# Windowed attention on one core: the row maxima transposed ahead of the values, and their rows sent by ScalarE alone

## The reference

```python
qkv = x @ w_qkv
q, k, v = jnp.split(qkv, 3, axis=-1)
# to_win: [B, H=16, nw=16 windows, W=128, E=32]; k_ctx, v_ctx: the window before, itself, the one behind
scores = jnp.einsum('bhnqe,bhnke->bhnqk', q * scale, k_ctx)
scores = jnp.where(valid[None, None, :, None, :], scores, NEG)
attn = jax.nn.softmax(scores, axis=-1)
out = jnp.einsum('bhnqk,bhnke->bhnqe', attn, v_ctx)
...
x = x + _layernorm(_L0_attn_ref(_layernorm(x, axis=-1), L0_attn_w_qkv), axis=-1)
x = x + _layernorm(_L0_ffn_ref(_layernorm(x, axis=-1), L0_ffn_gate_w1, ...), axis=-1)
```

## Time and profile before

| what | value |
|---|---|
| runs | 2930.49, 2940.21, 2943.89 us (median 2940.21) |
| profiled execution | 2937.19 us, of it the span 2935.3 |
| granted clock of TensorE, mean | 0.993 of full speed |
| attention stage | about 560 to 1290 us |
| one step of it, burst to burst | 5.43 us (1060.94 to 1066.37) |

### The profile page before, as it was taken

How to read it: one execution, slowest core, us unless ns; L and a number is a source line. 1 busy time by engine, 2 the same in 40 slices (tenths; PEclk the granted TensorE clock), 3 DMA queues, 4 the chain that set the end, 5 groups by cost and what they waited for, 6 DMA issues and landing times.

```text
span 2935.3 us, 55438 instructions
## 1 busy us (share of the span) xinstructions
PE 2867.0 (98%) x20252; PEld 2378.8 (81%) x20252; DVE 1994.9 (68%) x3769; ACT 1727.5 (59%) x3385; POOL 853.4 (29%) x713
## 2 busy tenths in 40 slices
PE   8999999999999999989989999999999999999998
PEld 6888888788888887778767888788888888888886
DVE  5333333488888887888868766886768766796664
ACT  3222222377767776665636666866667666676666
POOL 1000000188888887974400000500005000040003
PEclk9999999999999999999989999999999999999999
DMA  6555555678788889959999866985769765895642
GB/s 215 184 174 171 183 186 194 221 191 199 196 198 199 198 201 216 227 180 399 389 394 333 286 208 207 354 319 200 254 212 404 265 205 199 289 399 196 232 137 86
DMA packets 361429, 697.10 MB, mean 237 GB/s; under 512 B 26576, under 2 KB 127056, under 8 KB 361184
## 3 DMA queue, kind: packets, MB, share of 16 engines
q1 hardware_dynamic: 335456, 629.63, 67.0%
q10 hardware_dynamic: 17424, 32.24, 3.1%
q0 software_dynamic: 8304, 31.98, 2.7%
HBM read 525.45 MB, written 167.78 MB: 236 GB/s over the span
## 4 chain that ended last, share of the span: by engine, by line
PE 83%; DMA 6%; DVE 4%; issue 3%; ACT 2%; POOL 2%; ACTq 0%; DVEq 0%; SPq 0%; POOLq 0%
PE a_acc L571 18%; PE e_acc L1407 7%; PE e_hid L1390 7%; PE e_hid L1391 7%; PE e_hid L1392 7%; PE e_acc L1409 7%; PE e_acc L1408 7%; PE a_ps_score L622 5%; PE a_ps_keys L641 5%; PE a_ps_out L670 5%; DMA a_q_st<-a_max_rows 3%; DMA a_gate_att<-o_scratch 3%; PE a_ps_out L678 2%; PE a_ps_turn L688 1%; POOL a_gate_x L1231 1%
## 5 line engine op out<-in xcount | busy, mean ns | idle before, releaser
L1780 DVE SCALAR_TENSOR_TENSOR e_part<-e_ring,e_g_cols,e_part 128x512 f32<-128x512 f32 x896 | 647.5, 778 | 5.7 <-DMA e_ring<-mix_rows 3.2
L487 DVE TENSOR_REDUCE a_neg_max<-a_ps_score 128x1 f32<-128x384 f32 (+1 forms) x1024 | 490.1, 526 | 48.8 <-PE a_ps_score L622 47.5
L323 POOL TENSOR_TENSOR a_total<-a_probs 128x512 f32<-128x512 f32 x256 | 323.8, 1281 | 591.5 <-ACT a_probs L415 591.2
L415 ACT ACTIVATE a_probs<-a_ps_keys 128x384 f32<-128x384 f32 (+1 forms) x1024 | 422.8, 477 | 46.3 <-PE a_ps_keys L641 22.8
L1804 DVE TENSOR_TENSOR e_u_lo<-e_u,e_u_hi 128x512 fp32r<-128x512 f32 x256 | 180.0, 703 | 372.8 <-ACT e_u_hi L1538 372.6
L1534 ACT ACTIVATE e_u<-e_hid,e_mb 128x512 f32<-128x512 f32 x256 | 176.9, 691 | 432.0 <-PE e_hid L1392 419.4
L1263 POOL TENSOR_SCALAR e_var<-e_moments 128x4 f32<-128x4 f32 x15 | 6.7, 445 | 1273.4 <-DVE e_moments L1816 1272.7
L622 PE MATMUL a_ps_score<-a_k_st,a_q_st 96*128 96x384 f32 (+1 forms) x1024 | 332.5, 359 | 3.7 <-DMA a_q_st<-qk_scratch 2.8
L641 PE MATMUL a_ps_keys<-a_q_st,a_k_st 97*128 97x384 f32 (+1 forms) x1024 | 318.8, 353 | 12.3 <-DMA a_q_st<-a_max_rows 11.2
L333 POOL TENSOR_TENSOR a_total<-a_total,a_probs 128x512 f32<-128x512 f32 x224 | 286.3, 1281 | 58.0 <-ACT a_probs L415 55.5
L467 DVE TENSOR_TENSOR a_qk<-a_acc,a_qk 128x512 fp32r<-128x512 f32 x128 | 88.1, 690 | 308.1 <-ACT a_qk L364 308.1
(11 more groups left out here) (154 smaller groups left out, 6465.8 us busy)
## 6 DMA issues: line engine op xcount, KB each, us to landing
e_ring<-mix_rows SPq DMA_DIRECT2D x558, 512.0 KB, 5.5
qk_scratch<-a_qk SPq DMA_DIRECT2D x128, 512.0 KB, 3.3
a_k_st<-qk_scratch SPq DMA_DIRECT2D x180, 256.0 KB, 4.4
a_q_st<-qk_scratch SPq DMA_DIRECT2D x180, 256.0 KB, 4.4
v_scratch<-a_v SPq DMA_DIRECT2D x64, 256.0 KB, 3.1
a_v_sb<-v_scratch SPq DMA_DIRECT2D x64, 256.0 KB, 5.0
o_scratch<-a_out SPq DMA_DIRECT2D x128, 128.0 KB, 3.1
x_scratch<-a_gate_x POOLq DMA_DIRECT2D x16, 1024.0 KB, 10.2
```

Source lines behind the costliest of these rows:

```text
L323: add = pool.tensor_tensor(total[:, g % 2, i], p[0], p[1], ALU.add)
L415: act.activation(probs[:, m % PROBS, h, 0:(hi - lo) * WIN], ps_keys[x % TRIO][:, 0:(hi - lo) * WIN], ACT.Exp, scale=SCALE).then_inc(exp_do ...
L487: dve.tensor_reduce(neg_max[:, g % 2, i, h:h + 1], ps_score[y % TRIO][:, 0:(hi - lo) * WIN], AX_X, ALU.max, negate=True).then_inc(reduced, 1)
L1780: dve.scalar_tensor_tensor(out=part[:, n % 2, half, :], in0=ring[:, slot, :], scalar=g_cols[:, b, e:e + 1], in1=so_far, op0=ALU.mult, op1= ...
```

## The change

`turn_max` moves ahead of the burst, and its output goes to the first 128 columns of the bank of `ps_keys` that k0 of the same step used, in place of `ps_turn` (`turned_max`; in the first two only, which run ahead of the loop, it is still `ps_turn`). For that it waits for e0, which empties the bank, and k3, which writes the bank next, waits for `copy_rows`. `copy_rows` stands behind r0 in place of r2. Both rows are sent by ACT, between e2 and copy_out; SP sends none in the loop. `turn_max` no longer waits for `normalise`, nor `turn_out` for `copy_rows`, as they share no bank. `normalise` is cut in two: `invert`, the reciprocal, stands ahead of r7, the multiplication behind it.

```diff
--- before.py
+++ after.py
@@ -189,6 +189,12 @@
         def load_k(eng, n, c):
             load_stack(eng, n, c, k_st, 1, (0, 0, 1), k_loaded)
 
+        def turned_max(g):
+
+            if g < AHEAD - 1:
+                return ps_turn[0:2 * QH, 0, :]
+            return ps_keys[UNITS * (g - AHEAD + 1) % TRIO][0:2 * QH, 0:WIN]
+
         def send_row(eng, g, i):
             w = 2 * (g % HALF) + i
             eng.wait_ge(rows_done, g + 1)
@@ -275,8 +281,6 @@
                 if T >= 5 and T % 2 == 1 and n + 1 < ROUNDS:
                     sp.wait_ge(pv_done, T - 2)
                     load_v(n + 1, c)
-                if there(T + AHEAD - 1):
-                    send_row(sp, T + AHEAD - 1, 1)
                 if T == 0:
                     sp.wait_ge(v_done, TILES * (CHUNKS + 1))
                     for p in range(2):
@@ -426,13 +430,14 @@
                 for x in range(3):
                     if there(T):
                         weights(T, x)
+                if there(T + AHEAD - 1):
+                    for i in range(2):
+                        send_row(act, T + AHEAD - 1, i)
                 if there(T - LAG):
                     copy_out(T - LAG)
                 for x in range(3, UNITS):
                     if there(T):
                         weights(T, x)
-                    if x == 4 and there(T + AHEAD - 1):
-                        send_row(act, T + AHEAD - 1, 0)
                 along(T)
 
         def vector(dve, along):
@@ -492,11 +497,13 @@
                     for i in range(2):
                         dve.wait_ge(rows_landed[i][g % 2], 16 * (g // 2))
                 dve.wait_ge(max_turned, g + 1)
-                dve.tensor_copy(max_rows[:, g % 2, :], ps_turn[0:2 * QH, 0, :]).then_inc(rows_done, 1)
-
-            def normalise(g):
+                dve.tensor_copy(max_rows[:, g % 2, :], turned_max(g)).then_inc(rows_done, 1)
+
+            def invert(g):
                 dve.wait_ge(out_turned, g + 1)
                 dve.reciprocal(inv_sum[:, g % 2], ps_turn[:, 3, :].rearrange("p (h e) -> p e h", e=E)[:, 0:2, :]).then_inc(inv_done, 1)
+
+            def normalise(g):
                 dve.wait_ge(inv_done, g + 1)
                 if g >= 2:
                     dve.wait_ge(out_stored[g % 2], 16 * (g // 2))
@@ -543,13 +550,16 @@
                     copy_rows(1)
             for T in range(STEPS + LAG):
                 if there(T + AHEAD):
-                    for s in range(3):
-                        reduce(T + AHEAD, s)
+                    reduce(T + AHEAD, 0)
                 if there(T + AHEAD - 1):
                     copy_rows(T + AHEAD - 1)
                 if there(T + AHEAD):
-                    for s in range(3, UNITS):
+                    for s in range(1, UNITS - 1):
                         reduce(T + AHEAD, s)
+                if there(T - LAG):
+                    invert(T - LAG)
+                if there(T + AHEAD):
+                    reduce(T + AHEAD, UNITS - 1)
                 if there(T - LAG):
                     normalise(T - LAG)
                 along(T)
@@ -633,6 +643,8 @@
                     pe.wait_ge(rows_landed[1][g % 2], 16 * (g // 2 + 1))
                 if x == QH and g % HALF != HALF - 1:
                     pe.wait_ge(rows_landed[0][(g + 1) % 2], 16 * ((g + 1) // 2 + 1))
+                if x == TRIO and there(g + AHEAD - 1):
+                    pe.wait_ge(rows_done, g + AHEAD)
                 x += 8 * g
                 if x >= TRIO:
                     pe.wait_ge(exp_done, x - TRIO + 1)
@@ -643,10 +655,9 @@
 
             def turn_max(g):
                 pe.wait_ge(reduced, UNITS * (g + 1))
-                turned = g - AHEAD - LAG + 1
-                if turned > 0:
-                    pe.wait_ge(norm_done, turned)
-                pe.transpose(ps_turn[0:2 * QH, 0, :], neg_max[:, g % 2].rearrange("p w h -> p (w h)"), ident[:, :])\
+                if g >= AHEAD - 1:
+                    pe.wait_ge(exp_done, UNITS * (g - AHEAD + 1) + 1)
+                pe.transpose(turned_max(g), neg_max[:, g % 2].rearrange("p w h -> p (w h)"), ident[:, :])\
                   .then_inc(max_turned, 1)
 
             def values(g):
@@ -681,7 +692,6 @@
 
             def turn_out(g):
                 pe.wait_ge(out_copied, g + 1)
-                pe.wait_ge(rows_done, min(g + LAG + AHEAD, STEPS))
                 if g >= 1:
                     pe.wait_ge(norm_done, g)
                 for i in range(3):
@@ -736,12 +746,12 @@
                 scores(T, [1])
                 all_keys(T, [1, 2])
                 scores(T, [2])
+                if there(T + AHEAD - 1):
+                    turn_max(T + AHEAD - 1)
                 if there(T - LAG):
                     values(T - LAG)
                     sums(T - LAG)
                 along(T)
-                if there(T + AHEAD - 1):
-                    turn_max(T + AHEAD - 1)
                 scores(T, [3])
                 all_keys(T, [3])
                 scores(T, [4])
```

## The result

The changed kernel takes **2947.7 us** (median of 20 runs, 2941.4 to 2953.2), the kernel before, on the same chip, 2935.7 (20 runs). The ratio is 1.004, with a 95% interval of 1.0032 to 1.0048. So it is slower, by 12 us. One of the 20 executions of the kernel before took 3717.0 us and is left out of the ratio. The time lies within the range given (2917 to 2960) and within my bound of 0.5%, but the step from before to after went the other way: I had forecast -0.1%, and -3 us became +12. The profiled execution took 2945.94 us, its span 2944.1.

What follows compares the result with a forecast made beforehand. TensorE's step was bound by a loop through burst, turn, DVE's copy, r3, r7 and s2, plus rarer row waits. Terms -7.5 + 3 + 1 + 1 = -2.5 gave 2934.7 profiled, 2937 us median; range 2917 to 2960.

Steps and rivals of the forecast that it cites:

- The turn ahead of the burst: TensorE, turn between s2 and the burst: costs +0.11 us a step, bounds 0 and +0.31, e0's wait adding a few hundredths.
- The copy leaves the loop: DVE, ordinary steps: free of the copy, r3 can start at 1063.32 instead of 1063.45, -0.13 us a step.
- The reciprocal enters the loop: DVE, reciprocal ahead of r7: r7 starts 1.98 to 2.05 us behind r3 instead of 1.93, taken as +0.05 a step.
- Rows sent earlier: TensorE's waits at k4: maxima rows issued 2.4 us earlier, waits mostly go, -7.5 us, ends 0 and -13.
- The late steps: End of the attention: ACT's 0.83 us tile delays e0 and so the burst in seven steps, taken as +1 us.
- The statistics' delay of copy_out: Some twelve late steps: DVE's statistics delay both issues by 0.7 us and copy_out about 0.3; +1 us, ends 0 and +4.
- Row 1 to ACT: ACT's queue between e2 and copy_out: row 1's issue moved from SP costs 0, with 0.3 us of cover left.
- k3's wait: TensorE at k3: waits for a copy done about two microseconds before, so 0.
- B: Rival: the turn hides in the idle gap ahead of the burst, -8 us over 100 steps, 2926 or 2923; chance 0.20.
- C: Rival: the turn opens a second gap of 0.20 us between s2 and itself, about +22, giving 2959; chance 0.18.
- D: Rival: rows land as late as before, so the 7.5 us gain does not come, 2945; chance 0.11.

Runs made afterwards that it cites:

- e2: Not a run: one of ACT's exponentials in a step of the kernel; the changed kernel sends both rows between it and copy_out. No time or ratio belongs to it.
- k0 first: TensorE makes k0 of a step ahead of s0: on the changed kernel 2934.6 us, ratio 1.0002; on the kernel before, as control, 2934.9 us, 1.0006.
- k0 late: The changed kernel with k0 behind s1 in place of behind s0: 2983.7 us, ratio 1.0171 to the kernel before.
- the reciprocal back behind r7: The changed kernel with the reciprocal returned behind r7, the rest of the change kept: 2945.3 us, ratio 1.0040 to the kernel before.
- the reciprocal split off: The kernel before with only the reciprocal moved ahead of r7: 2933.2 us, ratio 0.9994.
- the tile moved: The kernel before with ACT's woven work of the last steps moved into the burst, ahead of copy_out: 2934.0 us, ratio 0.9996.
- the same, reciprocal back: The changed kernel with k0 ahead of s0 and the reciprocal returned behind r7: 2933.2 us, ratio 0.9993 to the kernel before.
- the same, reciprocal back and tile moved: The changed kernel with k0 ahead of s0, the reciprocal behind r7 and ACT's late tile inside the burst: 2931.6 us, ratio 0.9991 to the kernel before.

## Why the prediction was wrong

**Failed: "The turn ahead of the burst", +0.11 a step.** It measured +0.26 (from s2's load to the burst, 0.38 to 0.64). The row that I took, was the right one for the turn's own price: with k0 first it is 0.10. What failed was the comparison of e0's wait with it. I had e0 end at 1060.82 and the turn load 0.05 behind, at 1060.87, and end 0.03 later than without the wait, "a few hundredths more". With the burst 0.07 ahead of the turn's end, that sum gives 0.05 + 0.27 - 0.07 = 0.25 from e0's end to the burst. The runs show 0.11 to 0.12 from e0's end to the turn's load, and 0.23 from there to the burst: 0.34, in 90 of 102 steps of after and in all with k0 late, and never less than that with k0 first. The 0.09 between the two is most of the 0.10 by which a step was missed. In before e0 ended 0.12 ahead of the burst in the step read the earlier trace rows, and 0.09 in the median. The whole step can be told by e0 too. Before, e0 ends 5.34 behind a burst's start and the next burst follows 0.09 later: 5.43. After, it ends 5.23 behind it, and the next follows 0.35 later: 5.58. The comparison to make was this one: 0.34 needed where 0.09 to 0.12 stood. The rows for e0, before and then after (the bursts at 1066.37 and 1075.14):

```profile
1065.79 0.49 ACT L415 ACTIVATE a_probs<-a_ps_keys 128x384 f32<-128x384 f32 x1
```

```profile
1074.30 0.49 ACT L419 ACTIVATE a_probs<-a_ps_keys 128x384 f32<-128x384 f32 x1
```

**Right: "The copy leaves the loop", -0.13.** r3 came 0.15 earlier behind the burst in the step read. It is likely what lets e0 end 0.11 earlier, as s6 waits for r3; no run took it alone. **"The reciprocal enters the loop", +0.05:** it measured 0. s2's load is 2.58 behind r3 where it was 2.54 in the steps read, but that isn't the reciprocal's doing: the median is 2.56 in after and 2.56 with the reciprocal back behind r7. What adds the 0.02 to 0.04 stays open. (4 x 0.46 is 1.84, not 1.86, and r7 did start 1.98 behind r3 as forecast; what I left out is that it would be shorter.) A step: -0.15 + 0.04 + 0.26 = +0.15, against +0.03 in the forecast; the mean over the round is +0.13.

**Half right: "Rows sent earlier", -7.5.** The waits went as forecast, and loads of q took part of it back, 2.6 us. At 0.13 a step, 104 steps should cost 13.5; after is 8.7 late at T=104, so nearly 5 were gained up to there by this pair of profiles. Before's own 4.3 of waits ahead of 1130 is the highest of four: its controls (k0 first, the reciprocal split off, the tile moved) have 1.7, 1.5 and 2.9. Against the mean of the four, after is 10.6 late at T=104, which leaves 3. Between T=104 and T=127 the steps lose nothing on balance (8.7 behind becomes 6.4 behind).

**Right in kind: "The late steps".** ACT's tile makes the turn wait, 2.6 us in six steps against a term of +1. The statistics' delay of copy_out, +1, came in small: in five late steps of after (T=106, 108, 119, 123, 124) copy_out starts 0.10 behind the second issue's end, 2.17 to 2.22 behind the burst, so 0.15 to 0.20 late; in the others it follows the sums by less than 0.1. Its cost is under 1 us, as an estimate from these five. **Row 1 to ACT and k3's wait,** 0 each: nothing in the runs speaks against it (k3 is named once, with 0.2 us).

Sum by measured terms: +0.13 x 100 = +13, -4 to -7 for the rows, +2 to +3 for the late steps: +8 to +12; the profiled executions differ by 8.8, the medians by 12. This sum is made afterwards and is no test. (In the forecast's own sum, 2934.7 + 3.0 is 2937.7, and not 2937.)

**The rivals.** B (the turn hides): fell; idle time of 0.18 to 0.26 ahead of the burst before is still 0.15 to 0.25 in after and 0.15 to 0.27 with k0 first, and the turn's 0.10 comes on top. The Trainium skill (TensorEngine Tiling (Array Packing), Key Properties) says that switching the tiling mode drains TensorE; the gaps ahead of the burst agree, and so do those behind it, 0.20 in all three kernels. C: its sign came, and its sentence "a late e0 ... would give the same sign" named the cause, but the second gap of its own that carried its price of 0.20 doesn't exist. The sign that I gave for it, a gap ahead of the turn's load, came too: such a gap alone doesn't tell a drain from a wait. D: fell, as no row is waited for. The Trainium skill's 2.0 us for a DMA's fixed part (DMA: Bandwidth & Descriptors, the table of the two cost components), given for another path, is shown by no run here for a row alone.

**Open.** How much time the rows' earlier place is worth. Their waits, 9.2 to 12.0 us in before and its three controls, vanish with every early send. The times at which k0 starts, one profile of each:

| start of k0, us | T=104 | T=127 | from there to the end |
|---|---|---|---|
| before | 1130.9 | 1272.7 | 1662.7 |
| before, k0 first | 1128.1 | 1274.1 | 1659.4 |
| before, reciprocal ahead of r7 | 1127.6 | 1267.8 | 1663.1 |
| before, tile moved | 1129.4 | 1267.4 | 1662.4 |
| after, k0 first | 1126.6 | 1262.7 | 1664.2 |
| the same, reciprocal back | 1129.4 | 1269.1 | 1662.5 |
| the same, reciprocal back and tile moved | 1126.9 | 1263.4 | 1670.3 |

With the rows early and e0 out of the way, the attention ends some 5 us earlier in the mean (1265.1 against 1270.5), with ranges that overlap. What follows it takes 1659 to 1670 us and covers that: the medians are equal (1.0002, 0.9993 and 0.9991 against 1.0006, 0.9994 and 0.9996). Behind 1130 loads of q, POOL and the tile take turns as what is waited for. Whether the 5 us are lost by chance or by something behind the attention stays open.

## What to carry to other kernels

When a wait is put in front of the instruction that opens a dense stretch, take the releaser's end in the old trace, add the distance that such a handover and the instruction need (here 0.11 + 0.23), and compare with the stretch's start: what is missing is paid in each step unless the releaser's own work can be moved up, which here was one line. Take the releaser's end from many steps: one step had 0.12 where the median was 0.09. An issue of a DMA was not free on an engine that computes: in ACT's idle time two cost nothing in an ordinary step, amid its exponentials they cost 0.6 us a step. And a busy share of nearly 1 on TensorE hid 0.13 us in each step; count what was done in the stretch instead.

## What was not expected of the hardware

- From ACT's end to TensorE's load behind a wait for it: 0.11 to 0.12 us, in all 102 steps of after and of k0 late, and in 90 of 102 with k0 first. In the timeline it stands as idle time put down to "issue", or to another engine that had long been done.
- A DMA issue on ACT runs beside the exponential ahead of it, as its 0.60 begin with that one's start (1125.13 and 1125.15); the second in a row did not, and held the next exponential up until 0.05 behind its end.
- A reduction behind a reciprocal was shorter (0.52 to 0.53 against 0.56 in the medians), so that a reciprocal of 0.20 between two of them moved the end of the second by nothing.
- DMA engines at a share of 0.84 had no room left for six loads of 512 KB within 11 steps (T=60 to 70): the 24 steps around them took 4.5 us longer with k0 first, 9.7 in before.
